# A 3x3 convolution inside a fused attention and convolution kernel: from F(2,3) to F(4,3) along the columns, with GpSimd pooling two of the inputs

## The reference, cut to what matters

```python
x = x + attention(group_norm(x))          # window attention on 2x2 windows, and attention to 256 pooled keys
y = x
m = mask(group_norm(y))                   # per channel, from the centre of mass of the normalised image
x = y + conv3x3(maximum(group_norm(y) * m, 0), weight) + bias      # 256 -> 256 channels, padding 1
```

## Time and profile before

| what | us |
|---|---|
| three runs | 348.88, 350.37, 351.10 |
| median | 350.37 |
| span of the profiled execution | 347.5 |
| TensorE busy | 315.2 (91%) |
| VectorE busy | 272.5 (78%) |
| ScalarE busy | 148.8 (43%) |
| GpSimd busy | 83.0 (24%) |

### The profile page before, as it was taken

The page is one execution under the profiler, slowest core; times in us unless marked ns, Lnnn a source line. Parts: engine busy times, 40 slices in busy tenths (PEclk is TensorE's granted clock), DMA queues, the critical chain, the costliest instruction groups (busy, mean ns, idle before and its releaser), DMA issues.

```text
span 347.5 us, 4162 instructions
## 1 busy us (share of the span) xinstructions
PE 315.2 (91%) x1566; PEld 222.3 (64%) x1566; DVE 272.5 (78%) x488; ACT 148.8 (43%) x189; POOL 83.0 (24%) x46
## 2 busy tenths in 40 slices
PE   0879968999979999999799999999799999999995
PEld 0566344267866663688567744888388727877884
DVE  4996668769999586889989767799887847897572
ACT  2442548464490843554047855351165423031300
POOL 2088513440436020003910200008600200202000
PEclk9999968899989999999999999999999999999999
DMA  8779500009700000099011200197001000101002
GB/s 276 276 102 140 228 5 0 2 1 134 94 0 4 2 1 2 0 130 159 1 63 41 82 1 2 35 128 128 4 0 62 0 0 5 58 0 62 0 0 121
DMA packets 12068, 20.38 MB, mean 59 GB/s; under 512 B 2065, under 2 KB 8081, under 8 KB 11793
## 3 DMA queue, kind: packets, MB, share of 16 engines
q1 hardware_dynamic: 12048, 20.13, 28.2%
HBM read 7.93 MB, written 4.19 MB: 35 GB/s over the span
## 4 chain that ended last, share of the span: by engine, by line
PE 58%; DVE 23%; ACT 8%; issue 6%; POOL 3%; DMA 2%; SPq 0%; DVEq 0%; POOLq 0%
PE slot L1113 29%; PE cps L1145 15%; PE slot L1189 7%; DVE l_max L848 3%; PE cps L1113 3%; DVE mask L784 3%; PE cps L1189 2%; ACT probs L563 2%; POOL probs L379 2%; DVE v_lo L814 1%; DMA xy<-x 1%; PE slot L1392 1%; ACT xn_hi L452 1%; ACT p_w L608 1%; DVE xn L740 1%
## 5 line engine op out<-in xcount | busy, mean ns | idle before, releaser
L1145 PE MATMUL cps<-v_hi,cw_hi 128*128 128x512 f32 (+1 forms) x144 | 57.6, 400 | 3.5 <-DVE v_lo L814 2.9
L1145 PE MATMUL cps<-v_hi,cw_lo 128*128 128x512 f32 (+1 forms) x144 | 57.9, 402 | 0.0
L1145 PE MATMUL cps<-v_lo,cw_hi 128*128 128x512 f32 (+1 forms) x144 | 56.4, 392 | 0.0
L379 POOL TENSOR_TENSOR probs<-q_w,k_w 128x1024 f32<-128x1024 f32 x14 | 32.9, 2376 | 79.5 <-DVE rw L777 72.3
L848 DVE TENSOR_REDUCE l_max<-slot 128x4 f32<-128x1024 f32 x32 | 37.1, 1216 | 5.9 <-PE slot L1113 5.9
L563 ACT ACTIVATE probs<-slot 128x1024 f32<-128x1024 f32 x32 | 31.4, 1021 | 16.0 <-PE slot L1113 15.9
L1145 PEld LDWEIGHTS cps<-v_hi,cw_hi 128*128 128x128 f32 x144 | 27.4, 191 | 12.7 <-issue 5.2
L1145 PEld LDWEIGHTS cps<-v_hi,cw_lo 128*128 128x128 f32 x144 | 27.4, 190 | 7.4 <-issue 2.2
L1145 PEld LDWEIGHTS cps<-v_lo,cw_hi 128*128 128x128 f32 x144 | 27.4, 190 | 5.0
L362 POOL TENSOR_TENSOR mask<-rw 128x1024 f32<-128x1024 f32 x8 | 15.2, 1912 | 56.6 <-DVE rw L777 56.6
L1113 PE MATMUL slot<-xn_hi,w_hi 128*128 128x512 f32 (+1 forms) x68 | 27.3, 401 | 1.1 <-ACT xn_hi L452 1.1
(11 more groups left out here) (197 smaller groups left out, 635.0 us busy)
## 6 DMA issues: line engine op xcount, KB each, us to landing
xy<-x SPq DMA_DIRECT2D x8, 512.0 KB, 6.6
out<-xy SPq DMA_DIRECT2D x8, 512.0 KB, 2.6
qs<-probs SPq DMA_DIRECT2D x12, 256.0 KB, 5.8
qs<-probs SPq DMA_DIRECT2D x24, 128.0 KB, 8.3
raw_cw<-conv_w SPq DMA_DIRECT2D x2, 1152.0 KB, 6.4
ks<-probs SPq DMA_DIRECT2D x12, 128.0 KB, 6.9
probs<-h_qkv SPq DMA_DIRECT2D x2, 192.0 KB, 3.8
probs<-l_kv SPq DMA_DIRECT2D x2, 128.0 KB, 3.7
```

The source lines that it names most:

```text
L379: nc.gpsimd.tensor_tensor(product(b, j).rearrange("p (n w) -> p n w", n=NW), q_w[:].rearrange("p (n w) -> p n w", n=NW), k_w[:, j * G:(j + ...
L1145: ins = nc.tensor.matmul(cps[:, pos % 2, y0 * WT:y1 * WT], (cw_hi, cw_hi, cw_lo)[part][:, k, pos, dy + 1, o * P:(o + 1) * P], (v_hi, v_lo, ...
```

## The change

The convolution becomes F(4,3): four neighbouring outputs from six products. The six positions are three groups of two sides: NEAR, FAR and EDGE. A tile of a position has 256 columns (248 at the edge rows), and TensorE needs 216 such matmuls per image, where it needed 144 of 512. An event now holds both output tiles of one position side by side in one bank: 6 events of 36 matmuls per image. `conv.more` counts in the new, shorter matmuls, and the tables are set anew.

The input gets a pad column at either side (`pad`); a group takes 3 or 4 VectorE instructions (`combine`). Adding an event to the image takes 1 to 3 instructions, since most positions go into several of the four outputs with different factors, and the bias is now added by ScalarE (`add_bias`). The weights are 1.5 times as many; six positions are derived from three taps by VectorE for `k` = 0 and by GpSimd for `k` = 1 (`near_weights`, `far_weights`, `low_weights`). To make room the high tiles have two rotating slots, mask and pooled input lie in `probs`, and raw weights in `qkv_w`. Pooling for images 2 and 3 moves to GpSimd (`pooling_after`). The loads of image 2 wait until the first image's `pv` is done, and image 3 is loaded once more, early, for its moments.

```diff
-EARLY = 8
-REST = (4, 3, 5, 3, 4, 8)
-FRONT = (0, 11, 0, 0, 4, 3, 3, 3, 3, 3, 6, 10, 18)
-POOL_WAIT = 8
+EARLY = 12
+REST = (6, 5, 8, 5, 6, 12)
+FRONT = (0, 17, 0, 0, 6, 4, 4, 4, 4, 4, 9, 15)
+POOL_WAIT = 12
...
+            def low_weights():
+
+                link, t, far = weights, taps[1], cw_new[:, 1, FAR]
+                for k in (1, 0):
+                    pool.wait_ge(cw_act, 6 - k)
+                    for i in range(2):
+                        link(weight_low(nc.gpsimd, k, NEAR, i))
+                pool.wait_ge(soft_c, N_SOFT)
+                link(nc.gpsimd.tensor_scalar(far[:, 1], t[:, 2], 4.0, 0.0, ALU.mult, ALU.add))
...
+            def pooling_after(b):
+
+                link = Chain(pool, pool_c, N_POOL, pooled_by(b + 1))
+                pool.wait_ge(lnorm, b + 1)
+                pool.wait_ge(xn_ready, (b + 2) * KT)
+                link(nc.gpsimd.tensor_tensor(pool_t, xn[:, :, 0:2 * G], xn[:, :, 2 * G:4 * G], ALU.add))
+                link(nc.gpsimd.tensor_tensor(pool_s, pool_t[:, :, 0:G], pool_t[:, :, G:2 * G], ALU.add))
+                link(nc.gpsimd.tensor_copy(pool_hi[:], pool_s))
+                link(nc.gpsimd.tensor_tensor(pool_lo[:], pool_s, pool_hi[:].bitcast(F32), ALU.subtract))
...
                 if b == 1:
-                    mask_sum(0, 2)
-                    pool.wait_ge(v_dve, KT)
+                    mask_sum(0)
+                    pool.wait_ge(v_dve, 1)
                     pool.wait_ge(lv_pe, 1)
                 products(b)
...
+            def combine(rows, to, g):
...
+                if g == NEAR:
+                    nc.vector.scalar_tensor_tensor(to[:, 0], columns(1), -4.0, columns(3), ALU.mult, ALU.add)
+                    tile_step(nc.vector.scalar_tensor_tensor(to[:, 1], columns(2), -4.0, columns(4), ALU.mult, ALU.add))
+                    tile_step(nc.vector.tensor_tensor(to[:, 1], to[:, 1], to[:, 0], ALU.subtract))
+                    last = nc.vector.scalar_tensor_tensor(to[:, 0], to[:, 0], 2.0, to[:, 1], ALU.mult, ALU.add)
...
+            def conv_result(b, e):
...
+                if e == 0:
+                    ins = into(odd, 2.0, twice(m))
+                elif e == 1:
+                    into(y[:, 1], 0.5, m)
+                    ins = into(y[:, 3], 2.0, m)
...
                     query_lo(b)
                     key_lo(b)
                     dve.wait_ge(y_ready, b * KT)
+                    older_result(2)
+                    conv_low(older, EDGE)
                     row_sums(b - 1)
                     column_sums(b - 1)
                     normalisation(b - 1, 1)
                     mask_parts(b - 1)
                 maxima(b, range(6))
-                older_result(V_SUM)
+                older_result(3)
                 maxima(b, range(6, NB))
                 maxima_parts(b)
-                older_result(V_DIFF)
                 if not first:
                     for k in range(KT):
                         masked_image(b - 1, k)
-                    conv_tiles(b - 1, 0, 0)
+                    pad(b - 1)
+                    conv_tiles(b - 1, NEAR)
                 window_maxima(b)()
-                if not first:
-                    conv_tiles(b - 1, 1, 0)
-                older_result(V_LEFT)
+                older_result(4)
                 if not first:
-                    for k in range(KT):
-                        conv_low(b - 1, k, 0)
-                    for k in range(KT):
-                        conv_tiles(b - 1, k, 1)
-                older_result(V_RIGHT)
+                    conv_low(b - 1, NEAR)
+                    conv_tiles(b - 1, FAR)
+                older_result(5)
                 if not first:
-                    for k in range(KT):
-                        conv_low(b - 1, k, 1)
+                    conv_tiles(b - 1, EDGE)
+                    conv_low(b - 1, FAR)
```

More of the change, by code:

```diff
@@ L304, in step @@
                     stack(b + 1)
+                    stack_maxima(b + 1)
+                if b + 1 == RING - 1:
+                    sp.wait_ge(ssum_pe, b + 2)
+                    for k in range(KT):
+                        sp.dma_start(early[:, k], x[RING, k]).then_inc(early_in[k], 16)
                 if not first:
                     store(b - 1, 0)
-                if not last:
-                    stack_maxima(b + 1)
                 reload = b + RING - 1 < B and not first
@@ L398, in inner_weights @@
[L398 to L409 removed]
+            weights = Chain(pool, cw_pool, CW_POOL, 0)
@@ L1029, in step @@
                 residual(b, 1, 2)
-                if not first:
-                    pooling(b + 1)
-                if not first:
-                    conv_result(b - 1, (V_RIGHT,) if b == 1 else (V_LEFT, V_RIGHT))
                 if first:
@@ L1042, in last_front @@
                 dve.wait_ge(y_ready, B * KT)
-                conv_result(older, (V_LEFT, V_RIGHT))
+                conv_result(older, 2)
+                conv_low(older, EDGE)
                 row_sums(b, slice(0, 1))
@@ L1054, in last_front @@
+                last_low(0, NEAR)
+                last_tiles(0, FAR)
                 column_sums(b, slice(1, 2), mask_last[1])
-                conv_tiles(b, 0, 1)
-                conv_result(older, (POS + V_LEFT, POS + V_RIGHT))
-                conv_low(b, 0, 1)
+                last_low(0, FAR)
+                last_tiles(0, EDGE)
+                conv_result(older, 5)
                 mask_parts(b, slice(1, 2), mask_last[1])
+                last_low(0, EDGE)
                 masked_image(b, 1)
-                for phase in range(2):
-                    conv_tiles(b, 1, phase)
-                    conv_low(b, 1, phase)
+                pad(b, range(1, 2))
@@ L1142, in more @@
-                        if begin:
-                            wait_count(pe, conv_out, b * EVENTS + o * POS + pos - 1)
-                        y0, y1 = max(0, -dy), min(H, H - dy)
-                        ins = nc.tensor.matmul(cps[:, pos % 2, y0 * WT:y1 * WT],
-                                               (cw_hi, cw_hi, cw_lo)[part][:, k, pos, dy + 1, o * P:(o + 1) * P],
-                                               (v_hi, v_lo, v_hi)[part][:, k, pos, (y0 + dy) * WT:(y1 + dy) * WT],
-                                               start=begin and pos < 2, stop=end, skip_group_check=pos >= 2)
```

562 lines of the change are left out of this document (338 added, 224 removed).

## The result

The changed kernel takes 418.8 us in the median of 4 runs (416.7 to 421.9), the kernel before 350.1 on the same chip: a ratio of 1.198, 95% interval 1.191 to 1.205. It is slower, as forecast, but by 68.7 us where 17 were forecast, and far outside the range that ended at 373. Medians from here on leave out runs that are over 1.5% above the fastest of their kernel.

What follows compares the result with a forecast made beforehand. TensorE's and VectorE's stretches were taken to alternate as the bound. The 347.5 us span plus 5.0, 3.5, 3.3, 1.2 and 4.1 gave 364.6; with 2.9 for the median, 367.5 us, 4.9% slower, range 351 to 373.

Steps and rivals of the forecast that it cites:

- VectorE's work: Per image, VectorE's results, transformed inputs and low parts were priced at 18.5 us after the change against 14.6 before.
- what would prove it wrong: Far weights at 0.96 each, undisturbed VectorE overlap with GpSimd's products, or strided image sums costing over 0.6 per 512.
- Start-up: VectorE's and GpSimd's weight instructions collide from 48.2, delaying the first `pv` product: +5.0, bounds 0 and +7.
- round of image 1: GpSimd's products hold up VectorE's FAR instructions and a low part, delaying the next sums by head: +3.5, bounds +1 and +6.
- round of image 2: Convolution of image 1 begins 5.5 later, then shorter matmuls give back 2.2: +3.3, bounds -2 and +5.
- round of image 3: Convolution of image 2 begins 3.1 later, then shorter matmuls give back 1.9: +1.2, bounds -2 and +5.
- last stage: Later row sums, image 3 and results: VectorE ends at 348.5 instead of 344.4, +4.1, bounds 0 and +7.
- (a) to (d): Rounds 2 and 3: GpSimd pooling shifts `key_lo` (1.2 later, 0.3 earlier); work before row sums +3.0; results +0.4; NEAR wait +0.9.
- (d): Rounds of images 2 and 3: the NEAR group waits for both rectified tiles, where the first went ahead before: +0.9.
- (e): Last stage: 13 addition instructions per output tile, 12 us for both, starting at 336.6; VectorE ends at 348.5.
- TensorE's saving: Convolution matmuls fall from 130.8 us to 98.9, at 0.1145 per 256 columns: 31.9 us less, nearly all going into waiting.
- The rivals: Engines hardly meet, 356.6 (0.20); gains and losses cancel, 352.5 (0.10); TensorE stays bound, 328 (0.09); matmuls not cheap, 383+ (0.03).

Runs made afterwards that it cites:

- The measuring kernels: Two kernels computing nothing of the reference, timing instructions at different steps between elements: VectorE f32 512 elements took 1.048 us at step 4.
- The dense kernel: Changed kernel with image additions and tile inputs on neighbouring columns instead of every fourth, output columns misplaced: 375.8 us, ratio 1.074 to the kernel before.
- the best dense kernel: Changed kernel with dense additions and tile inputs, pooling on VectorE and GpSimd's far weights later, output columns misplaced: 371.2 us, ratio 1.061 to the kernel before.
- the one kernel made for it: 20 unread 512-column matmuls per image added where TensorE waits, to a whole-computing version of the change (387.6 us): 390.6 us, ratio 1.115.

## Why the prediction was wrong

**The step of the prediction that failed is the price in "VectorE's work": "one of 512 takes 0.68, so 0.60 behind another", taken for instructions that touch every fourth column.** The row was of a step of 2. With a step of 4 they take 1.09, and 1.0 behind another. The text named this among what would prove it wrong, and carried no bound for it: a step of 4 is an access that the trace of before doesn't show, and I priced it as if it did. The affected instructions of the changed kernel are 24 x 0.41 + 6 x 0.83 + 20 x 0.18 + 4 x 0.40 + 2 x 0.81 = 21.6 us of additions, and 18 x 0.41 + 3 x 0.84 + 2 x 0.41 + 12 x 0.20 = 13.1 of tile inputs. Their sum, 34.8, is about what VectorE lost when the columns were made dense (34.0), and that gave some 40 us of time.

The Trainium skill has a rule on it that I did not weigh (Advanced Engine Details and Errata, "SBUF Cachelines"): lines of 16 bytes, full speed only with at least two hits on a line. The measuring kernels agree for f32 on VectorE (step 2, two hits in 16 bytes: free; steps 4 and 8, one: 0.37 and 0.39 more; step 3 between them) and on ScalarE (1.045 to 2.01). They don't agree for bf16 written by VectorE, where step 4 still hits each 16 bytes twice and takes 1.325 for 0.686, nor for GpSimd's writes, which show no price at step 4.

**Start-up** (forecast +5.0, measured +9.0). The port's part is right. The far weights lasted 1.46 to 2.47, the first `pv` product started at 59.95 for 58; moving GpSimd's wait brought it to 55.68 (from the second far weight, L965, to it: 7.9 and 3.9). The Trainium skill's lock (SBUF — State Buffer, "Who interferes with whom") fits here and in isolation, where only instructions with two sources in SBUF waited. What lies above the forecast is in good part spread. Six kernels that share the changed start-up reached the first sums by head at 64.9 to 68.0 us (mean 66.6, granted clock to there 0.83 to 0.91), and three that share the old one at 59.0 to 61.9 (mean 60.8, 0.89 to 0.94): 5.8 apart, and 7.5 at the end of these sums, so that the 9.0 sets an early execution of the one beside a late one of the other. Eight kernels that start GpSimd's far weights later reach it at 62.5 to 64.5 (mean 63.4; the one with matmuls added in the start-up, 66.6, left out): the waits for GpSimd were worth some 3 of the 5.

**The rounds.** The dense kernel has no step of 4 and all other parts of the change, as the forecast had it. By stage, the surplus over the kernel before:

| stage | forecast | changed | dense | dense, pooling on VectorE, far weights later |
|---|---|---|---|---|
| to the sums of image 0 | 5.0 | 9.0 | 6.0 | 3.5 |
| round of image 1 | 3.5 | 15.4 | 8.3 | 10.1 |
| round of image 2 | 3.3 | 11.5 | 4.4 | 3.6 |
| round of image 3 | 1.2 | 16.6 | 5.0 | 1.3 |
| last stage | 4.1 | 14.9 | 3.2 | 3.2 |
| sum | 17.1 | 67.4 | 26.9 | 21.7 |

(The marks are 65.0, 144.5, 221.9, 301.6, 374.4, and 62.5, 143.8, 220.4, 296.4, 369.2.) With dense columns, the terms for image 2 and the last stage hold within about 1 us. That for image 3 was too small by 3.8 in the dense kernel (pooling on VectorE takes this away). Part of it is the sum: (a) to (d) of that round give 4.0, and the text took 3.1 without saying why (d) is left out. That for image 1 was too small by 5. The products did meet VectorE's FAR instructions as described, 2.76 each:

```profile
114.68 2.76 DVE L919 SCALAR_TENSOR_TENSOR v_new<-v_new 128x512 f32<-128x512 f32 x1
117.47 2.76 DVE L920 SCALAR_TENSOR_TENSOR v_new<-v_new 128x512 f32<-128x512 f32 x1
122.42 3.40 DVE L941 SCALAR_TENSOR_TENSOR v_lo<-v_new,v_hi 128x1024 fp32r<-128x1024 f32 x1
```

But a wait that took this away did not shorten the dense kernel's round (83.2 with it, 81.3 without), so the port alone does not set that round's length. The round keeps a granted clock of 0.88 against 0.95; what bounds it is not settled.

**The last stage.** (e) said 13 additions per output tile in 12 us for both, VectorE 5 us behind TensorE. They took 18.6 (the row of 22 is named by the shape of its first; 20 of them have 256 elements):

```profile
392.96 2.03 DVE L1240 TENSOR_TENSOR xy<-xy,slot 128x1024 f32<-128x1024 f32 x1
399.06 12.50 DVE L1019 SCALAR_TENSOR_TENSOR xy<-slot,xy 128x512 f32<-128x512 f32 x22
```

VectorE ends at 411.6, TensorE's last matmul starts at 401.5. With dense columns the same additions run from 358.82 to 370.67, 11.9 us, as the forecast had it:

```profile
362.51 8.16 DVE L1019 SCALAR_TENSOR_TENSOR xy<-slot,xy 128x512 f32<-128x512 f32 x22
```

In this stage VectorE is 13.2 us less busy when dense, and the stage is 11.7 shorter: where VectorE ends the program, the price of the step counts nearly in full.

**TensorE's saving** was sized rightly (0.115 measured, 0.1145 taken), and rightly said to go into waiting; the run with 216 more matmuls fits it, since giving 25 us of it back cost nothing, though at a higher granted clock. What I did not see is that with these waits the granted clock is lower too (0.862 for 0.979): the sum held every TensorE term at full clock. Between the changed kernel and the dense one the granted clock rose by 0.055, which fits time falling by more than VectorE's busy time. Clock and time move together in an unchanged program too: in the kernel before, on one chip, 347.0 us goes with 0.985 and 351.5 with 0.971. That the clock is a cause and not only a companion was not shown: the one kernel made for it hardly moved the clock.

**The rivals.** All four gave less than the forecast save the last (383 and more, for matmuls that don't get cheap), and its mechanism did not happen. No case had a larger loss by VectorE. The moved and added loads, costed at nothing, are not the loss: TensorE waits 2.0 us for DMA after, 1.9 before.

**What stays open.** 21 us between the best dense kernel (371.2) and the kernel before. There 25 us of TensorE's work cost 11.7 and 10 us of VectorE's nothing. It is neither engine's load alone, as far as these two runs show; about half of it lies in the round of image 1.

## What to carry to other kernels

Before pricing an instruction by a row, compare how both walk memory, not only shape and type: if the edit changes the step between neighbouring elements and no row shows that step, it is an unknown cost with bounds of its own. An algorithm that saves multiplications by cutting rows into more interleaved parts pays for it in the engine that splits and joins them; when several parts take the same product, put them innermost. When TensorE ceases to be the bound, work taken off it may give nothing back, and its granted clock may fall on top.

## What was unexpected of the hardware

- f32 in SBUF on VectorE, 512 elements: 0.682 at steps 1 and 2, 0.825 at 3, 1.048 at 4, 1.067 at 8; within 0.03 of that for a stepped read, two stepped reads or a stepped write.
- ScalarE pays more for step 4, read or written (1.045 to 2.01 per 1024), GpSimd nothing for a write at it (1.260 to 1.275 per 512).
- VectorE writing bf16 from f32 sources: 0.686 at step 1, 1.325 at step 4, 2.594 at step 8.
- At 1.2 GHz convolution matmuls of 256 columns stand 0.21 to 0.23 apart, about what 512 columns need at 2.4 (0.227): over a stretch at the lower level the saving is gone.
